# Decoder layer: the gated MLP product and the normalisation of the weighted sums on GpSimd, layer norm statistics on ScalarE, self output rows one cell later

## The chip, the cores and the metric

One core of a Trainium2 chip. Its engines are TensorE (PE in the profile, its weight loads PEld), VectorE (DVE), ScalarE (ACT), GpSimd (POOL) and SyncE (SP), which only issues DMAs here. Each has its own instruction queue and runs it in order; they meet in semaphores. The metric is the device time of one execution in microseconds, as the median of several.

## What is computed

A decoder layer in fp32 on x, 8 sequences of 512 rows by 512, with a context of the same shape. It is cut here to what matters; H = 16 heads of 32 columns, and the weights come in as they are named.

```python
x = x + self_attn(ln(x))        # q, k, v = ln(x) @ W_attn + b; q, k normed per head; causal softmax
x = x + cross_attn(ln(x), ctx)  # per row and head: the 32 largest of 512 scores, softmax over these alone
x = x + mlp(ln(x))              # below; act_quant rounds each row to 127 steps of its largest entry

def ln(x):                      # no gain, no bias
    m, v = mean(x), var(x)
    return (x - m) / sqrt(v + 1e-5)

def mlp(x):                     # w_gate, w_up: 2048 x 512, w_down: 512 x 2048, all rounded to -1, 0, 1 times a scale
    gate = silu(act_quant(x) @ w_gate.T)
    up = act_quant(x) @ w_up.T
    return act_quant(gate * up) @ w_down.T
```

## The kernel before

**Slots and cells.** One software pipeline runs over 168 slots, s = -7 to 160. Slot s works on query tile s of self attention (128 rows, one group of 4 heads: 4 tiles times 4 groups are 16 slots for each of 8 sequences) and, LAG = 20 slots later, on the same tile of cross attention. Slots repeat with a period of 16, called a batch here, and "slot 14" means s modulo 16; it begins where VectorE begins its list for s. Each slot has 8 cells, self and cross in turn, one head each. TensorE does in a cell: transposes of a head's probabilities (L595), a head's scores (L627 or L632), the weighted sum of the head before (L609), and then the shared units that `cells(s)` puts into this cell: projections for the next group (self_qkv, cross_kT, cross_v, cross_qT), the MLP's gate, up, hT and down, the output projections self_out and cross_out (L656) with the transposes ahead of them (self_oT, cross_oT), and transposes of normed rows ("feed", "x2T"). Shared units alternate between two PSUM banks, so a unit waits until the one two before it has been read. ScalarE copies each transposed block, each score block and each unit out of PSUM, cell by cell in the same order, and does the exponentials between.

**VectorE's list in a slot** is written out by hand (the loop at the end of its block). For each of the 4 cross heads it finds the 32 largest scores in 4 rounds of a maximum (L878) and a replacement (L883), in two halves of two heads, FIRST_MAX and ROUND_1 to ROUND_3, and the rest lies between: self maxima (smx), the normalisation `norms` of the finished sums (L900 reciprocal of the softmax denominators, L909 two products, so and co), `mlp` (L968 the product of silu(gate) and up into hh, L971 its row maximum), the row scale, `cross_rows` and `self_rows` (L926, L939: projection plus residual, then the statistics L929, L942 and aggregation L931, L946), `feed_stats_of` (L1000), `down` (L989). An MLP chunk is 512 of 2048 inner columns of a row tile; a tile has an early and a late chunk in each of two slots and its down projection in a third. The late chunk is worked on in the next slot, behind ROUND_1. VectorE's replacement of round 0 waits until GpSimd has done with cW of the slot before.

**GpSimd's list in a slot**: the biases cnb and snb (the negated maxima), the late chunk's silu (th, hh: L1115, L1117), the subtraction of head 2 and 3 (cS minus cW, L1170), low parts of the split operands (L1163), row quantisation, the quantisation of the inner rows (`inner_quant`, L1126, L1129, which TensorE's hT waits for), the low part of cell 3's unit, biases again, the early chunk's silu, `squares`, `head_norm` (L1146, L1149 a power, L1154; once in 4 slots, in slots 2, 6, 10 and 14), the subtraction of heads 0 and 1, and the layer norms of rows. A layer norm is four one-column instructions and a pass over 512 columns (L1049 to L1057).

**Chain around a group of heads.** In slots 2, 6, 10 and 14 TensorE forms cross_kT in cell 0 and cross_qT in cell 3; ScalarE reads each twice; GpSimd forms the low part; SyncE copies the parts into place with 8 times 4 DMAs per pair; the next slot's scores read them.

## Time and profile before

| | |
|---|---|
| time, median of 3 runs (lowest to highest) | 4032.62 us (4030.38 to 4032.80) |
| profiled execution, its time | 4034.79 us |
| its span | 4033.0 us |
| TensorE busy | 3329.4 us, 83%, 18502 matmuls |
| VectorE busy | 3343.9 us, 83% |
| ScalarE busy | 2450.5 us, 61% |
| GpSimd busy | 1796.7 us, 45% |

The span is what the trace covers; the rest of the execution's time lies around it. The first 300 us prepare weights and start the pipeline, self attention alone runs until about 425 us, six steady batches lie between 704 and 3365 us, then self attention ends, and the last 133 us hold only MLP work. A busy TensorE is not one at its peak, since its time depends on the granted clock, and a share over the whole span says little about which engine is late in a slot.

### The profile page before, as it was taken

The page shows a single profiled execution, that of the slowest core. Times are in us where ns is not written, and L with a number is a line of the kernel's source. Part 1 is how long each engine was busy: PE and PEld are TensorE (multiplying, and loading weights), DVE is VectorE, ACT ScalarE, POOL GpSimd, SP SyncE. Part 2 cuts the span into 40 slices and gives each one's busy share as a digit, 9 for nine tenths or more (in the row PEclk, how much of TensorE's full clock was granted, in tenths as well). Part 3 has the DMA queues.
Part 4 walks back from the last instruction along what each step waited for, and adds up shares of the span by engine and source line. Part 5 has one row for each costly group of instructions (what it writes and reads, how often), then busy time and mean ns, then how long its engine had stood idle before and what let it go on. Part 6 is the DMA issues. An engine that isn't in the chain of part 4 may idle for free.

```text
span 4033.0 us, 61337 instructions
## 1 busy us (share of the span) xinstructions
PE 3329.4 (83%) x18502; PEld 2434.3 (60%) x18502; DVE 3343.9 (83%) x7699; ACT 2450.5 (61%) x4921; POOL 1796.7 (45%) x2316
## 2 busy tenths in 40 slices
PE   2587898998989898998899888997899888877775
PEld 2365576666666666666666666666666666555542
DVE  4312299999999899899989999999989999999962
ACT  3344476666766567666766676666766676455533
POOL 0123244445654555444544555445544554344433
PEclk7768888888988899888988898898988898877767
DMA  7122322322222212222223222222232221211100
GB/s 271 52 54 64 99 64 76 84 77 60 77 77 72 70 49 79 79 73 69 74 77 84 63 71 67 74 65 62 77 89 79 58 66 43 61 45 35 32 21 19
DMA packets 167443, 283.04 MB, mean 70 GB/s; under 512 B 40639, under 2 KB 52939, under 8 KB 166606
## 3 DMA queue, kind: packets, MB, share of 16 engines
q1 hardware_dynamic: 160782, 275.98, 25.1%
q10 hardware_dynamic: 6336, 3.15, 0.3%
q8 instruction: 153, 2.51, 0.3%
q14 instruction: 172, 1.41, 0.1%
HBM read 113.27 MB, written 31.46 MB: 36 GB/s over the span
## 4 chain that ended last, share of the span: by engine, by line
DVE 40%; PE 25%; POOL 13%; issue 11%; ACT 4%; SPq 3%; DMA 1%; DVEq 0%; POOLq 0%; ACTq 0%
DVE cW L883 17%; DVE top L878 13%; PE bank L684 5%; PE bank L656 4%; PE bank L609 4%; POOL srs L1149 4%; SPq L513 3%; PE bank L672 2%; DVE smx L1019 2%; PE bank L637 2%; POOL cS L1170 2%; PE bank L595 2%; DVE hh L968 2%; POOL hh L1117 1%; DVE hmx L971 1%
## 5 line engine op out<-in xcount | busy, mean ns | idle before, releaser
L883 DVE MATCH_REPLACE8 cW<-top,cW 128x512 f32<-128x512 f32 x1536 | 1026.8, 676 | 0.0
L878 DVE MAX8 top<-cW 128x8 f32<-128x512 f32 x1536 | 981.4, 681 | 0.0
L799 ACT ACTIVATE PT<-bank 128x512 f32<-128x512 f32 (+3 forms) x1024 | 537.9, 525 | 356.5 <-PE bank L595 353.1
L1170 POOL TENSOR_TENSOR cS<-cS,cW 128x512 f32<-128x512 f32 x512 | 667.7, 1325 | 185.4 <-ACT cW L827 185.3
L609 PE MATMUL bank<-cv,PT 128*128 128x33 f32 x4096 | 585.0, 290 | 138.7 <-ACT PT L799 138.1
L609 PEld LDWEIGHTS bank<-cv,PT 128*128 128x128 f32 x4096 | 552.8, 209 | 176.5 <-ACT PT L799 170.2
L1177 POOL TENSOR_SCALAR cnb<-top 128x2 f32<-128x2 f32 x256 | 49.0, 191 | 938.1 <-DVE top L878 924.3
L609 PEld LDWEIGHTS bank<-sv,PT 128*128 128x128 f32 x2560 | 397.4, 211 | 82.2 <-ACT PT L799 59.6
L827 ACT ACTIVATE cW<-cW,cnb 128x512 f32<-128x512 f32 x512 | 348.7, 737 | 110.5 <-DVE cW L883 110.3
L684 PE MATMUL bank<-w_group,xT 128*128 128x384 f32 x1024 | 411.6, 550 | 0.0
L609 PE MATMUL bank<-sv,PT 128*128 128x33 f32 x2560 | 373.3, 280 | 36.7 <-ACT PT L799 35.6
L595 PE MATMUL bank<-ident,cS 128*128 128x128 f32 x2048 | 350.1, 298 | 63.2 <-POOL cS L1170 63.2
L821 ACT ACTIVATE cS<-cS,cnb 128x512 f32<-128x512 f32 x512 | 379.6, 741 | 16.1 <-DVE cW L883 16.1
L1019 DVE TENSOR_REDUCE smx<-sP 128x2 f32<-128x256 f32 (+3 forms) x256 | 205.9, 804 | 212.7 <-ACT sP L808 212.7
L1163 POOL TENSOR_TENSOR part<-part 128x512 fp32r<-128x512 f32 x128 | 168.3, 1315 | 451.1 <-ACT part L742 450.9
L595 PEld LDWEIGHTS bank<-ident,cS 128*128 128x128 f32 x2048 | 279.9, 162 | 116.7 <-POOL cS L1170 67.3
L883 DVE MATCH_REPLACE8 cW<-top,cS 128x512 f32<-128x512 f32 x512 | 342.5, 677 | 0.0
L878 DVE MAX8 top<-cS 128x8 f32<-128x512 f32 x512 | 327.2, 681 | 5.7 <-ACT cS L808 5.7
L814 ACT ACTIVATE sP<-sP,snb 128x384 f32<-128x384 f32 (+3 forms) x512 | 294.9, 578 | 35.5 <-POOL snb L1184 34.8
L808 ACT ACTIVATE cS<-bank 128x512 f32<-128x512 f32 x512 | 311.8, 609 | 1.6 <-PE bank L632 1.6
L684 PEld LDWEIGHTS bank<-w_group,xT 128*128 128x128 f32 x1024 | 205.2, 211 | 137.2 <-issue 40.3
L632 PE MATMUL bank<-ck_stack,cq_stack 128*128 128x512 f32 x512 | 269.1, 526 | 5.8 <-ACT cS L808 4.4
(151 smaller groups left out, 6092.4 us busy)
## 6 DMA issues: line engine op xcount, KB each, us to landing
sk_stack<-part SPq DMA_DIRECT2D x512, 64.0 KB, 2.0
sq_stack<-part SPq DMA_DIRECT2D x512, 64.0 KB, 2.0
ck_stack<-part SPq DMA_DIRECT2D x512, 64.0 KB, 2.0
cq_stack<-part SPq DMA_DIRECT2D x512, 64.0 KB, 2.0
w_group<-wa_by_group SPq DMA_DIRECT2D x32, 768.0 KB, 4.5
w_group<-wc_by_group SPq DMA_DIRECT2D x32, 768.0 KB, 4.3
feed<-in_x SPq DMA_DIRECT2D x32, 256.0 KB, 2.9
feed<-in_ctx SPq DMA_DIRECT2D x32, 256.0 KB, 3.0
```

Of the source, the lines that this page charges most:

```text
L595: mm = pe.transpose(turned_ps[C.parity("turned_full", label)][:, k * P:(k + 1) * P], p[:, k * P:(k + 1) * P], ident[:])
L609: mm = pe.matmul(o[:, j * (HD + 1):(j + 1) * (HD + 1)], pt[:, k * P:(k + 1) * P], v[m // NT % len(v)][:, k, j, :], start=k == 0, stop=k == ...
L684: mm = pe.matmul(ps[:, 0:3 * P], xT[:, c, t * P:(t + 1) * P], w_group[:, c, :], start=False, stop=c == NC - 1, skip_group_check=True)
L799: act.activation(PT[k][:, 0:n], turned_ps[k][:, 0:n], ACT.Copy).then_inc(turned_read, step("turned_read", label))
L808: act.activation(dst, score_ps[k][:, 0:n], ACT.Copy).then_inc(score_read, step("score_read", label))
L814: act.activation(p, p, ACT.Exp, bias=snb[:, j:j + 1], scale=SCALE).then_inc(sexp, step("sexp", (m, j)))
L821: act.activation(cS[c % 2][j][:], cS[c % 2][j][:], ACT.Exp, bias=cnb[c % 2][:, j:j + 1], scale=SCALE).then_inc(cexp, step("cexp", (c, j)))
L827: act.activation(cW[j][:], cW[j][:], ACT.Exp, bias=cnb[c % 2][:, j:j + 1], scale=SCALE).then_inc(crest, step("crest", (c, j)))
L878: dve.max(top8[:, j, r, :], src[:]).then_inc(topk, step("topk", (c, r, "max", j)))
L883: dve.match_replace(cW[j][:], top8[:, j, r, :], src[:], REPLACED).then_inc(topk, step("topk", (c, r, "replace", j)))
L1019: dve.reduce_max(smx[:, 2 * half:2 * half + 2], sP[half][:, :, 0:n], AXX).then_inc(smax, step("smax", (s, half)))
L1170: pool.tensor_tensor(cS[m % 2][j][:], cS[m % 2][j][:], cW[j][:], ALU.subtract).then_inc(cprob, step("cprob", (m, j)))
```

## The change

- GpSimd takes the product of silu(gate) and up (third instruction of `silu`), early and late chunk; VectorE keeps the row maximum. ScalarE's next read of an up bank waits for GpSimd in place of VectorE.
- ScalarE copies both finished weighted sums and denominators from PSUM to a new SBUF tile oc (`copy_out`, cell 1). VectorE takes the reciprocals from there (`inverses`), GpSimd forms so and co (`normalise`), ahead of the subtraction of heads 2 and 3. TensorE may reuse the PSUM bank after the copy.
- The row statistics of all layer norms move to ScalarE: a copy with an accumulated sum, a tiny scaling to the negative mean, and a square with an accumulated sum. They stand in cells 4 and 5 (cross rows), 4 and 6 (feeds of the next slot), 6 and 7 (self rows). GpSimd's layer norm loses two one-column instructions.
- self_oT and self_out move from cells 2 and 3 to 3 and 4, the transpose of the x1 rows from cell 1 to 2, cross_qT from cell 3 to 4. VectorE's `self_rows` stands behind ROUND_1 of the second half. GpSimd handles the low parts of cells 3 and 4 together.
- SyncE stores a slot's rows and loads those of the next at the end of the slot, behind the copies of the parts, with the xres load last; feeds are loaded behind these. x1res is the same buffer as xres.

```diff
-        for at, cell, unit in ((1, 5, ("cross_v", g)), (2, 0, ("cross_kT", g)), (2, 3, ("cross_qT", g))):
+        for at, cell, unit in ((1, 5, ("cross_v", g)), (2, 0, ("cross_kT", g)), (2, 4, ("cross_qT", g))):
...
-        u[1].append(("feed", "x1", x1_tile(s)))
+        u[2].append(("feed", "x1", x1_tile(s)))
-        u[2].append(("self_oT", self_tile(s)))
-        u[3].append(("self_out", self_tile(s)))
+        u[3].append(("self_oT", self_tile(s)))
+        u[4].append(("self_out", self_tile(s)))
...
+            def row_stats_of(s, k):
+                out = []
+                if k in (4, 5) and cross_tile(s) is not None:
+                    out.append((("x2", cross_tile(s)), x2t, x2sum, (0, 1) if k == 4 else (2,)))
+                if k in (4, 6):
+                    for f in feeds(s + 1):
+                        if f[0] == "x":
+                            out.append((f, feed[ring[f] % RING], fsum[normed.index(f) % RING], (0, 1) if k == 4 else (2,)))
+                if k in (6, 7) and self_tile(s) is not None:
+                    out.append((("x1", self_tile(s)), xres, x1sum, (0, 1) if k == 6 else (2,)))
+                return out
...
+                        if on(s - 3) or on(s - LAG - 3):
+                            pe.wait_ge(out_copied, upto("out_copied", s - 1))
...
-                                act.wait_ge(h_dve, upto("h_dve", ("h", *prev)))
+                                act.wait_ge(h_pool, upto("h_pool", ("h", *prev)))
...
+                    def copy_out(s):
+                        m, c = s - 2, s - LAG - 2
+                        if not on(m) and not on(c):
+                            return
...
+                        o = out_ps[s % 2][:].rearrange("p (k n) -> p k n", k=2)
+                        act.activation(oc[:, first:last, :], o[:, first:last, 0:HG * (HD + 1)], ACT.Copy).then_inc(
+                            out_copied, step("out_copied", s))
+                    def statistics(s, k):
+                        for label, x_, sums_, steps in row_stats_of(s, k):
+                            if 0 in steps:
+                                if label[0] == "x2":
+                                    act.wait_ge(dve_rows, upto("dve_rows", label))
+                                elif label[0] == "x1":
+                                    act.wait_ge(x1_added, upto("x1_added", label[1]))
+                                    act.wait_ge(x1_norm, upto("x1_norm", (label[1] - 1, 2)))
+                                else:
+                                    act.wait_ge(feed_in[ring[label] % RING], upto(f"feed_in{ring[label] % RING}", label, 16))
+                                    p = normed.index(label)
+                                    if p >= RING:
+                                        act.wait_ge(feed_pool, upto("feed_pool", (normed[p - RING], 2)))
+                                if label[0] == "x2":
+                                    act.wait_ge(pool_rows, upto("pool_rows", ("ln", label[1] - 1, 3)))
+                                act.wait_ge(row_stats, upto("row_stats", (label, 0)) - 1)
+                                act.activation(junk[:], x_[:], ACT.Copy, accum_out=sums_[:, 0:1]).then_inc(
+                                    row_stats, step("row_stats", (label, 0)))
+                                act.wait_ge(row_stats, upto("row_stats", (label, 0)))
+                                act.activation(sums_[:, 1:2], sums_[:, 0:1], ACT.Copy, scale=-1.0 / D).then_inc(
+                                    row_stats, step("row_stats", (label, 1)))
+                            else:
+                                act.wait_ge(row_stats, upto("row_stats", (label, 2)) - 1)
+                                act.activation(junk[:], x_[:], ACT.Square, bias=sums_[:, 1:2], accum_out=sums_[:, 2:3]).then_inc(
+                                    row_stats, step("row_stats", (label, 2)))
...
-                        if on(m):
-                            dve.wait_ge(so_full, upto("so_full", m))
-                        if on(c):
-                            dve.wait_ge(co_full, upto("co_full", c))
+                        o = oc[:].rearrange("p k (h d) -> p k h d", h=HG)
+                        dve.wait_ge(out_copied, upto("out_copied", s))
                         dve.wait_ge(so_norm, upto("so_norm", m - 1))
                         dve.wait_ge(co_norm, upto("co_norm", c - 1))
                         dve.reciprocal(rr[:, first:last, :], o[:, first:last, :, HD]).then_inc(recip, step("recip", s))
-                        dve.wait_ge(recip, upto("recip", s))
-                        for k, n, o_t, unit in ((0, m, so, "self_oT"), (1, c, co, "cross_oT")):
-                            if not on(n):
-                                continue
...
-                            mult = dve.tensor_tensor(o_t[:, qt, g * P:(g + 1) * P].rearrange("p (h d) -> p h d", h=HG),
-                                                     o[:, k, :, 0:HD], rr[:, k, :].unsqueeze(2).to_broadcast([P, HG, HD]),
-                                                     ALU.mult)
...
...
-                        dve.wait_ge(dve_rows, upto("dve_rows", ("x2", t)))
-                        dve.bn_stats(mstat[:], x2t[:]).then_inc(dve_rows, step("dve_rows", ("stats", t)))
-                        dve.wait_ge(dve_rows, upto("dve_rows", ("stats", t)))
-                        dve.bn_aggr(mv[:], mstat[:]).then_inc(dve_rows, step("dve_rows", ("aggr", t)))
...
-                            dve.wait_ge(h_pool, upto("h_pool", ("r", t, n)))
-                            dve.wait_ge(shared_read, upto("shared_read", (("up", t, n), 0)))
-                            dve.tensor_tensor(hh[:, n, :], hh[:, n, :], uc[:], ALU.mult).then_inc(
-                                h_dve, step("h_dve", ("h", t, n)))
-                            dve.wait_ge(h_dve, upto("h_dve", ("h", t, n)))
+                            dve.wait_ge(h_pool, upto("h_pool", ("h", t, n)))
...
+                        top(c, 1, ROUND_1)
                         self_rows(s)
-                        top(c, 1, ROUND_1)
-                        feed_stats_of(s + 1)
...
-                    def layer_norm(dst, src, mvt, col, name, sem_, label, ready):
+                    def layer_norm(dst, src, sums_, col, name, sem_, label, ready):
 
                         ready()
-                        pool.tensor_scalar(col[:, 0:1], mvt[:, 1:2], 1.0, EPS, ALU.mult, ALU.add).then_inc(sem_, step(name, label(0)))
+                        pool.tensor_scalar(col[:, 0:1], sums_[:, 2:3], 1.0 / D, EPS, ALU.mult, ALU.add).then_inc(sem_, step(name, label(0)))
                         pool.wait_ge(sem_, upto(name, label(0)))
                         pool.tensor_tensor(col[:, 1:2], col[:, 0:1], minus_half[:, 0:1], ALU.pow).then_inc(sem_, step(name, label(1)))
                         pool.wait_ge(sem_, upto(name, label(1)))
-                        pool.tensor_tensor(col[:, 2:3], mvt[:, 0:1], col[:, 1:2], ALU.mult).then_inc(sem_, step(name, label(2)))
-                        pool.wait_ge(sem_, upto(name, label(2)))
-                        pool.tensor_scalar(col[:, 3:4], col[:, 2:3], -1.0, 0.0, ALU.mult, ALU.add).then_inc(sem_, step(name, label(3)))
-                        pool.wait_ge(sem_, upto(name, label(3)))
-                        return pool.tensor_scalar(dst, src, col[:, 1:2], col[:, 3:4], ALU.mult, ALU.add)
+                        return pool.tensor_scalar(dst, src, sums_[:, 1:2], col[:, 1:2], ALU.add, ALU.mult)
...
+                    def normalise(s):
+                        m, c = s - 2, s - LAG - 2
+                        o = oc[:].rearrange("p k (h d) -> p k h d", h=HG)
+                        for k, n, o_t, name in ((0, m, so, "self_oT"), (1, c, co, "cross_oT")):
+                            if not on(n):
+                                continue
+                            b, qt, g = n // SLOTS, n % NT, n // NT % NG
+                            pool.wait_ge(recip, upto("recip", s))
+                            if b and g == 0:
+                                pool.wait_ge(shared_full, upto("shared_full", (name, NT * (b - 1) + qt)))
+                            mult = pool.tensor_tensor(o_t[:, qt, g * P:(g + 1) * P].rearrange("p (h d) -> p h d", h=HG),
+                                                      o[:, k, :, 0:HD], rr[:, k, :].unsqueeze(2).to_broadcast([P, HG, HD]),
+                                                      ALU.mult)
+                            if k == 0:
+                                mult.then_inc(so_norm, step("so_norm", n))
+                            else:
+                                mult.then_inc(co_norm, step("co_norm", n))
...
+                            pool.wait_ge(h_pool, upto("h_pool", ("r", t, n)))
+                            pool.wait_ge(shared_read, upto("shared_read", (("up", t, n), 0)))
+                            pool.tensor_tensor(hh[:, n, :], hh[:, n, :], uc[:], ALU.mult).then_inc(
+                                h_pool, step("h_pool", ("h", t, n)))
...
+                        normalise(s)
                         for j in (2, 3):
                             probability(c - 1, j)
                         low_parts(now[0] + now[1] + now[2])
                         rows_quant(s)
                         inner_quant(s - 1)
-                        low_parts(now[3])
+                        low_parts(now[3] + now[4])
```

On VectorE, the second half of slot 14, from the end of the first half on. Before:

```order
L878 MAX top<-cW 128x8 x2
L883 MATCH_REPLACE cW<-top,cW 128x512 x2
L878 MAX top<-cS_2 128x8
L878 MAX top<-cS_3 128x8
L1019 TENSOR_REDUCE smx<-sP 128x2
L939 TENSOR_TENSOR xres<-bank,xres 128x512
L942 BN_STATS x1stat<-xres 128x6
L946 BN_AGGR x1mv<-x1stat 128x2
L883 MATCH_REPLACE cW<-top,cS_2 128x512
L883 MATCH_REPLACE cW<-top,cS_3 128x512
L878 MAX top<-cW 128x8 x2
L883 MATCH_REPLACE cW<-top,cW 128x512 x2
```

After:

```order
L943 MATCH_REPLACE cW<-top,cW 128x512 x2
L938 MAX top<-cS_2 128x8
L938 MAX top<-cS_3 128x8
L1032 TENSOR_REDUCE smx<-sP 128x2
L943 MATCH_REPLACE cW<-top,cS_2 128x512
L943 MATCH_REPLACE cW<-top,cS_3 128x512
L938 MAX top<-cW 128x8 x2
L976 TENSOR_TENSOR xres<-bank,xres 128x512
L943 MATCH_REPLACE cW<-top,cW 128x512 x2
L938 MAX top<-cW 128x8 x2
L998 TENSOR_REDUCE hmx<-hh 128x1
L943 MATCH_REPLACE cW<-top,cW 128x512 x2
```

The add of the self output moves behind the first replacement and maximum of this half, and the two statistics instructions behind it are gone.

On GpSimd, the start of slot 13 up to the quantisation of the inner rows (hcol, hh). Before:

```order
L1177 TENSOR_SCALAR cnb<-top 128x2
L1184 TENSOR_SCALAR snb<-smx 128x2
L1115 TENSOR_SCALAR th<-th 128x512
L1117 TENSOR_TENSOR hh<-th,hh 128x512
L1170 TENSOR_TENSOR cS_2<-cS_2,cW 128x512
L1170 TENSOR_TENSOR cS_3<-cS_3,cW 128x512
L1126 TENSOR_TENSOR hcol<-hcol,wscale 128x1
L1129 TENSOR_SCALAR hh<-hh,hcol 128x512 x4
```

After:

```order
L1208 TENSOR_SCALAR cnb<-top 128x2
L1215 TENSOR_SCALAR snb<-smx 128x2
L1142 TENSOR_SCALAR th<-th 128x512
L1144 TENSOR_TENSOR hh<-th,hh 128x512
L1148 TENSOR_TENSOR hh<-hh,uc 128x512
L1099 TENSOR_TENSOR so<-oc,rr 128x128
L1099 TENSOR_TENSOR co<-oc,rr 128x128
L1201 TENSOR_TENSOR cS_2<-cS_2,cW 128x512
L1201 TENSOR_TENSOR cS_3<-cS_3,cW 128x512
L1157 TENSOR_TENSOR hcol<-hcol,wscale 128x1
L1160 TENSOR_SCALAR hh<-hh,hcol 128x512 x4
```

Three instructions stand between the silu's second step and the subtraction of head 2 that weren't there.

On TensorE, slot 14, cells 2 to 4, from the transposes of probabilities of cell 2 on; cross_qT is the line with x1T, self_out those with ones and wproj. Before:

```order
L595 MATMUL bank<-ident,sP 128x128 x2
L627 MATMUL bank<-sk_stack,sq_stack 128x384
L629 MATMUL bank<-mask,ident 128x128
L609 MATMUL bank<-cv,PT 128x33 x4
L637 MATMUL bank<-ident,so 128x128 x4
L595 MATMUL bank<-ident,cS_1 128x128 x4
L632 MATMUL bank<-ck_stack,cq_stack 128x512
L609 MATMUL bank<-sv,PT 128x33 x2
L703 MATMUL bank<-x1T,w_group 128x512 x4
L653 MATMUL bank<-bias,ones 128x512
L656 MATMUL bank<-wproj,oT 128x512 x4
L595 MATMUL bank<-ident,sP 128x128 x2
```

After:

```order
L610 MATMUL bank<-ident,cS_1 128x128 x4
L647 MATMUL bank<-ck_stack,cq_stack 128x512
L624 MATMUL bank<-sv,PT 128x33 x2
L652 MATMUL bank<-ident,so 128x128 x4
L610 MATMUL bank<-ident,sP 128x128 x2
L642 MATMUL bank<-sk_stack,sq_stack 128x384
L644 MATMUL bank<-mask,ident 128x128
L624 MATMUL bank<-cv,PT 128x33 x4
L718 MATMUL bank<-x1T,w_group 128x512 x4
L668 MATMUL bank<-bias,ones 128x512
L671 MATMUL bank<-wproj,oT 128x512 x4
```

The transpose of so follows cell 3's own work in place of cell 2's, and cross_qT and self_out follow cell 4's.

## Rows read from the trace of the kernel before

**Rows 1.** Stretches: us; busy PE, PEld, DVE, ACT, POOL; clock; DMA.

```profile
2478.00:2922.00 444.00, 392.51 (x2285) 289.66 (x2284) 409.13 (x946) 296.68 (x606) 225.54 (x289) 0.90 0.27 72
...
3700.00:3900.00 200.00, 141.26 (x637) 102.61 (x638) 189.17 (x448) 97.14 (x166) 73.14 (x86) 0.68 0.08 22
```

**Rows 2.** Timeline of DVE, slot 14 of two batches: start, duration, [idle before].

```profile
2490.11 0.69 DVE L939 TENSOR_TENSOR xres<-bank,xres 128x512 f32<-128x512 f32 x1 [4.95 <-PE bank L656]
...
2933.85 0.69 DVE L939 TENSOR_TENSOR xres<-bank,xres 128x512 f32<-128x512 f32 x1 [4.95 <-PE bank L656]
```

**Rows 3.** Waits of DVE, 2478 to 2922: us in total, times, longest.

```profile
DVE xres L939 <- PE bank L656: 13.9, 4, 5.6
DVE x2res L989 <- PE bank L672: 5.8, 4, 2.2
...
DVE cW L883 <- POOL cS L1170: 3.3, 3, 2.3
```

**Rows 4.** Waits of PE, the same stretch.

```profile
PE bank L637 <- POOL hh L1129: 19.6, 4, 8.7
PE bank L595 <- POOL cS L1170: 8.3, 3, 5.1
```

**Rows 5.** The chain of waits by line, the same stretch.

```profile
by line: DVE cW L883 15.9%; DVE top L878 12.4%; issue 11.3%; PE bank L684 5.6%; PE bank L609 5.5%; POOL srs L1149 4.9%; PE bank L656 4.5%; PE bank L595 3.1%; POOL cS L1170 3.1%; DVE smx L1019 2.6%; DVE hh L968 2.4%; PE bank L672 2.4%; PE ba
```

**Rows 6.** Groups of DVE instructions, the same stretch: busy us, mean ns, idle before.

```profile
L968 DVE TENSOR_TENSOR hh<-hh,uc 128x512 f32<-128x512 f32 x16 | 16.1, 1008 | 3.0 <-POOL hh L1117 3.0
...
L909 DVE TENSOR_TENSOR so<-bank,rr 128x128 f32<-128x128 f32 x16 | 4.7, 292 | 0.5
...
L942 DVE BATCH_NORM_STATS2 x1stat<-xres 128x6 f32<-128x512 f32 x4 | 2.8, 695 | 0.1
...
L946 DVE BATCH_NORM_AGGREGATE x1mv<-x1stat 128x2 f32<-128x6 f32 x4 | 0.7, 182 | 0.1
```

**Rows 7.** Timeline of POOL, start of a slot 13 to the quantisation.

```profile
2447.25 0.19 POOL L1184 TENSOR_SCALAR snb<-smx 128x2 f32<-128x2 f32 x1
2447.52 0.62 POOL L1115 TENSOR_SCALAR th<-th 128x512 f32<-128x512 f32 x1
2448.22 1.27 POOL L1117 TENSOR_TENSOR hh<-th,hh 128x512 f32<-128x512 f32 x1
2449.45 2.94 POOL L1170 TENSOR_TENSOR cS<-cS,cW 128x512 f32<-128x512 f32 x2
2452.64 0.19 POOL L1126 TENSOR_TENSOR hcol<-hcol,wscale 128x1 f32<-128x1 f32 x1 [0.26 <-DVE hcol L982]
```

**Rows 8.** Groups, whole span: a broadcast product, an ACT copy, the accumulator read.

```profile
L1154 POOL TENSOR_TENSOR sx<-sx,srs 128x1024 f32<-128x1024 f32 x32 | 62.0, 1937 | 2.5
...
L742 ACT ACTIVATE sx<-bank 128x256 f32<-128x256 f32 x128 | 48.9, 382 | 269.3 <-PE bank L684 268.9
...
L1398 ACT ACTIVATION_READ_ACCUMULATOR scratch<-wnat 128x1 f32 x12 | 2.3, 192 | 0.0
```

**Rows 9.** Timeline of POOL, slot 14: low part, power, subtraction.

```profile
2487.50 1.27 POOL L1163 TENSOR_TENSOR part<-part 128x512 fp32r<-128x512 f32 x1 [9.19 <-ACT part L742]
...
2491.52 5.45 POOL L1149 TENSOR_TENSOR srs<-srs,minus_half 128x32 f32<-128x32 f32 x1
...
2499.08 2.50 POOL L1170 TENSOR_TENSOR cS<-cS,cW 128x512 f32<-128x512 f32 x2
```

**Rows 10.** Timeline of DVE near the end: the product beside GpSimd, and alone.

```profile
3564.49 1.28 DVE L968 TENSOR_TENSOR hh<-hh,uc 128x512 f32<-128x512 f32 x1
...
4016.85 0.69 DVE L968 TENSOR_TENSOR hh<-hh,uc 128x512 f32<-128x512 f32 x1 [1.99 <-POOL hh L1117]
```

**Rows 11.** Timeline of PE, slots 13 to 15.

```profile
2453.65 1.09 PE L637 MATMUL bank<-ident,hh 128*128 128x128 f32 x4 [5.13 <-POOL hh L1129]
...
2489.91 0.38 PE L595 MATMUL bank<-ident,sP 128*128 128x128 f32 x2
...
2491.24 0.63 PE L595 MATMUL bank<-ident,cS 128*128 128x128 f32 x4
...
2500.40 0.66 PE L595 MATMUL bank<-ident,cS 128*128 128x128 f32 x4 [0.74 <-POOL cS L1170]
```

184 lines of the change are left out of this document (81 added, 103 removed).

## The prediction

> **What bounds the kernel now.** I read the table of stretches first. In a steady batch of 16 slots VectorE is busy 409 of 444 us, TensorE 393 at a mean granted clock of 0.90, ScalarE 297 and GpSimd 226 [rows 1]. So two engines are nearly full, and two have room. The period is 2933.85 - 2490.11 = 443.74 us, the distance of the same instruction in two batches [rows 2]. The engine waits come next: VectorE's largest is 13.9 us for the self output rows, then 5.8 us for the down projection and 3.3 us for GpSimd's subtraction [rows 3]; TensorE's are 19.6 us for the quantised MLP rows and 8.3 us for the same subtraction [rows 4]. Last the chain of waits: in this batch it is on VectorE's top-32 lines for 28% only, the rest is spread over TensorE lines and over GpSimd's power, 4.9% [rows 5]. The chain hops from engine to engine, so work taken from VectorE pays only in the stretches where VectorE is the one that is late. That is how I cost the change: engine by engine, along the chain.
>
> **What leaves VectorE.** Per batch: 16 multiplications by the up rows at 1.01 us (16.1 us), 32 normalising multiplications at 0.29 but 0.21 apart in the queue (6.6 us), 12 times statistics and aggregation, 0.70 + 0.18 less their overlap, 0.83 (10 us) [rows 6]. Sum 32.7 us per batch. That would be the gain if nothing else bound anything.
>
> **What the other engines get.** GpSimd's product of 512 columns is 1.27 us, with the gap to the next 1.35 [rows 7]; that is the price of each moved multiplication. The normalising product (128 columns, a broadcast operand) is not in the trace. Its nearest rows are the broadcast product of 1024 columns at 1.94 us and a two-column GpSimd instruction at 0.19 us [rows 7, 8]; on the line between them 128 columns cost 0.41. I take 0.41, with 0.19 and 0.62 (the one-input pass over 512 columns [rows 7]) as ends. Two of them and their gaps: 1.0 us per slot. Each layer norm loses two tiny GpSimd instructions, 0.55 us with gaps. ScalarE gets a copy of 264 columns from PSUM per slot, 0.38 as its copy of 256 [rows 8], and per tile two passes over 512 columns with an accumulator read of 0.19 each [rows 8] and one tiny one: about 0.6 + 0.19 twice, plus 0.25, 1.85 us, 12 times a batch. That is 28 us on an engine that has 147 us idle per batch, so by itself I cost it at nothing; what covers it is that ScalarE mostly waits for TensorE. If that cover is gone (the three feed tiles in one cell, 3 us at once) it costs a TensorE wait of 1 to 2 us.
>
> **A rule against the trace.** When a subtraction of two tiles on GpSimd overlaps VectorE's multiplication, the pair of them takes 2.94 us; alone it takes 2.50 [rows 7, 9]. VectorE's multiplication is 0.69 alone and 1.28 beside GpSimd [rows 10]. The top-32 instructions never show it. So I credit 0.45 us per late chunk to GpSimd once VectorE's two-input product is gone. The Trainium skill, page "SBUF — State Buffer", section "Who interferes with whom", says that a VectorE instruction with two SBUF inputs contends with a GpSimd instruction that reads SBUF and one with a single input does not; by it the relief is the one that I take from the rows. The page "Perfetto Trace Analysis", section "Optimizing Scalar/DVE Operations", warns that moving work between these two engines might not help; the rival that it stands for is priced below as B from rows.
>
> **The chain leg by leg, one batch.** Numbers are change against before; minus is gained.
>
> Slots 8 and 9, VectorE never waits. Two early multiplications (1.4 beside GpSimd, 0.7 alone), the norms of slot 8 (0.4), three feed statistics (2.8 with their gaps) and one late chunk. The late chunk pays little: VectorE (replacement, maximum, reciprocal) would be ready 2.7 us after its self maxima, GpSimd (bias, two silu steps, the new product) 3.6 us after them, by the steps of [rows 7]; so 0.9 us of the 1.4 for norms and product turns into a wait, and 0.5 is left. Sum -5.8.
>
> Slot 10 takes that back. Its quantisation hangs on GpSimd: from the bias at 2447.25 to the scale at 2452.64 that queue has 0.26 us of idle time in it, in slot 13's example [rows 7]. The new product (1.35) and the two norms (1.0), less 0.45 and less the wait, put the first quantised rows 1.7 us later; TensorE waits for them in every such slot, 5.13 us in this one [rows 11]. Then cross_qT comes a cell later. A cell's own work is 1.33 us at the full clock (2489.91 to 2491.24) [rows 11], and twice that at the lower of the two clock levels, 1.2 instead of 2.4 GHz, to which the granted clock has fallen after such a wait (four transposes take 1.09 there and 0.63 at the full level). Behind cross_qT hang ScalarE's read, GpSimd's low part, the head norm with its 5.45 us power and 1.95 us product, and the subtraction for head 0, which the next slot's VectorE and TensorE both need: GpSimd runs this without idle time from 2487.50 to 2501.6 [rows 9], and TensorE waits 0.74 for it [rows 11]. At the start of slot 11 I expect about +0.5: leg +6.3.
>
> Slots 11 and 12, VectorE again: two early (1.4), one late (0.5), norms (0.4), one feed (0.8): -3.1.
>
> Slot 13: quantisation, +1.7. Slot 14: cross_qT a cell later, +1.35, and the early product ahead of the head norm, +1.35; with the pair 2.8 to 2.9, I take +2.85 with its larger gap.
>
> Slot 15: the layer norm is shorter (-0.55), the early product is off VectorE (-0.7), the self output comes a cell later (+1.5 with its unit), but VectorE now does its replacement and maximum (2.5 us) before it waits and has no statistics after it (0.83): -3.35. Sum -3.1. In slot 14 the same gain is void, since GpSimd is late there.
>
> Slot 0: quantisation, +1.7. Slots 1 and 2: self output and norms, +1.5 - 3.35 - 0.4 = -2.25. Slots 3 and 4 are TensorE and the SyncE copies: 0.
>
> Slots 5 to 7: VectorE gains 3.9 up to the cross rows of slot 6 (norms 0.4, statistics 0.9, early product 1.0, and the late chunk of slot 6 in full, 1.6, since the sum of squares gives GpSimd time), but TensorE was waiting only 2.3 us for them, so -2.3; then cross_qT +1.5, the early product +1.35, layer norm -0.55, late product -0.5. Sum -0.5.
>
> Total: -5.8 + 6.3 - 3.1 + 1.7 + 2.85 - 3.1 + 1.7 - 2.25 - 0.5 = -2.2 us per batch. Six batches lie between 704 and 3365 us: -13. Ahead of them there is no MLP and SyncE's copies and TensorE lead; I put 0, within 5.
>
> **The end.** From 3426 to 3900 us only the cross attention and MLP run; VectorE is busy 189 of 200 us, TensorE 141 [rows 1], and there is no head norm. Here the saving comes through: 8 early multiplications at 0.9, 8 late ones at 0.5 (the 1.28 beside GpSimd [rows 10] becomes a wait for it), four row statistics 3.5, norms 2.4; less 1 for the down slots: -16. In the last 133 us nothing covers a hop. Per tile the last chunk's product is 1.35 on GpSimd for 0.70 on VectorE [rows 10]: +2.6 in four tiles; three layer norms whose sums come through ScalarE, about +1 each: +5.6 in all. Net -10.4.
>
> SyncE's list is the same in its order around the copies but that feeds are issued behind the row loads and that x1res shares the buffer of xres; the tiles of the two are slots apart, and I cost it at 0.
>
> **Sum.** -13 - 10.4 = -23.4 us, against the profiled execution's 4034.8 (its span is 4033.0 and 1.8 lie around it) that is 4011; against the median of 4032.6 it is 4009. I say 4010.
>
> **Rivals.** *A, the legs have slack.* If engines upstream of the q leg run so much earlier that its later cell doesn't show, the four q legs (6 us) and the quantisation (5 us) go: -13 per batch, -78 and the end's -10: about 3945. For it: only 8.3 us of waits per batch are put to the subtraction [rows 4]. Against: GpSimd has no idle time in that leg [rows 9]. The full 32.7 us cannot come: TensorE's 393 us and even half of its 51 us of idle time are more than the 411 that would be left.
>
> *B, GpSimd becomes the bound (slower).* If each q leg starts in the low clock (+2.7, not +1.35), and if the layer norm of the x1 rows, which must now wait for ScalarE's last cell and stands ahead of the next slot's biases, pushes silu and quantisation by 2 to 3 us in slots 15 and 0, a batch costs 4 x 1.35 + 3 - 2.2 = +6.2, six of them +37, the end -10: about 4060. It decides from +1.7 per batch on, where it eats the end's gain. For it: GpSimd's unbroken run [rows 9] and the 19.6 us that TensorE waits for quantised rows [rows 4]. Against: GpSimd is busy only 226 of 444 us [rows 1].
>
> *C, it only trades places.* Late chunks: VectorE waits where it worked, which I priced; if the early ones do the same, and legs and gains cancel, the time is 4033 within 8.
>
> **How the numbers follow.** Forecast (4010, own range 3985 to 4024) 0.40; A 0.12; C 0.19; B 0.29. The unknown product moves a quantisation leg by 0.4 either way, 1.2 per batch, 7 in all. The range holds A at its low end and B at its high end: 3945 to 4060. A measurement of this kernel can tell about 0.2% from no change. Faster by more: 0.40 + 0.12, rounded to 0.51; within: 0.20; slower: 0.29.
>
> **What would show it.** Right: a period near 441.5 in the middle; VectorE busy 377 of it with its waits up from 32 to about 60; TensorE's wait for the quantised rows up by 1.5 us a slot; the subtraction for heads 2 and 3 at 2.50 a pair; GpSimd's normalising product near 0.4 us; the power's start in slot 14 later against cross_kT by 2.8. A is right if the waits for the subtraction don't grow, B if they double and the clock's mean falls below 0.88. Wrong altogether: ScalarE copies of the transposed weights delayed by the statistics so that TensorE waits for them by more than 10 us a batch, or a GpSimd product beside the top-32 work that takes much more than 1.3 us.

## The result: slower by 2.6%

The changed kernel takes 4137.30 us in the median (4131.15 to 4139.49), the kernel before 4031.50 beside it: a ratio of 1.0261, interval 1.0243 to 1.0278. I had said 4010, with 4060 as the end of the range. The profiled executions have spans of 4133.7 and 4033.0 us. One execution of the kernel before and one of undo_cells took 5954 and 5998 us and stand apart from all others; without its own, the median of undo_cells is 4123.2 in place of the 4125.5 below.

A batch, 16 slots from one slot 4 to the next, in the table of stretches of the changed kernel (the columns of [rows 1]):

```profile
2255.70:2713.10 457.40, 403.12 (x2285) 298.81 (x2285) 376.10 (x874) 317.61 (x681) 245.90 (x312) 0.89 0.26 70
```

VectorE is busy 376 us where it was 409 [rows 1], as foretold (377). But the batch has become 13.5 us longer. VectorE's and TensorE's waits in it, against [rows 3] and [rows 4]:

```profile
DVE rr L956 <- ACT oc L858: 28.8, 12, 5.2
DVE x2res L1016 <- PE bank L687: 13.8, 4, 4.3
DVE hmx L998 <- POOL hh L1148: 13.1, 7, 3.8
DVE xres L976 <- PE bank L671: 11.6, 3, 8.7
DVE cW L943 <- POOL cS L1201: 7.8, 8, 2.5
...
PE bank L652 <- POOL hh L1160: 20.2, 4, 7.7
...
PE bank L610 <- POOL cS L1201: 12.2, 4, 5.0
```

VectorE now waits 81 us a batch where it waited 32. The largest wait is new: 28.8 us in 12 slots for ScalarE's copy of the weighted sums, ahead of the reciprocals. The second new one is 13.1 us for GpSimd's product. The chain of waits of the same stretch has moved off VectorE's top-32 lines, from 28% [rows 5] to 13%:

```profile
by line: issue 8.7%; PE bank L624 7.4%; DVE cW L943 7.3%; PE bank L699 6.9%; DVE top L938 5.8%; PE bank L671 5.3%; POOL cS L1201 4.1%; PE bank L610 4.1%; POOL srs L1180 3.6%; PE bank L687 3.1%; PE bank L718 3.1%; PE bank L652 3.0%; PE bank 
```

Where in the batch the time is: below are slot lengths, each the distance between VectorE's first maxima (top<-cS) of two slots, the median over five batches; for the other kernels the difference to before. They are worked out from the timelines of VectorE; the kernels after the second column are those of the experiments. Some slots jump between two lengths from batch to batch, so medians of slots do not add up to a batch: as the mean of the same five batches the bottom line would be +13.7, +2.0, +6.2, +2.7, -2.9, -5.2, -3.7 and -10.0.

```
slot   before   changed   undo_norm  copy_early    early_x1      q_back    no_cells    hh_stats hh_stats_x1
0        34.6      +6.8        +6.0        +6.9        +0.3        +1.4        -1.5        +4.8        -2.2
1        23.6      +0.8        -0.9        -0.2        -1.0        -1.0        -0.6        +0.2        -0.6
2        23.3      +1.8        +0.0        -0.1        -0.1        -0.1        -0.6        +0.0        +0.0
3        26.0      +1.3        +4.6        +4.1        +5.8        +4.6        +2.4        +1.3        +2.1
4-7     119.1      +0.4        +0.2        +0.5        -0.8        -1.1        -1.6        -1.4        -1.4
8-9      51.7      -4.0        -5.5        -5.3        -5.3        -5.3        -5.3        -5.5        -5.5
10       27.6      +6.5        +1.7        +4.0        +5.5        +3.1        +3.1        +2.7        +2.7
11-12    50.8      -0.2        -1.7        -2.3        -2.3        -2.5        -2.5        -2.8        -2.8
13       25.1      +2.6        -1.0        +0.9        +3.8        -0.5        -0.5        -1.0        -0.9
14       31.2      -3.2        -3.8        -3.5        -3.5        -3.6        -1.7        -1.9        -1.9
15       30.5      +0.8        +0.3        +1.0        +1.0        -1.0        +0.4        +0.4        +0.4
sum     443.4     +13.7         0.0        +6.0        +3.3        -6.0        -8.3        -3.2       -10.3
```

Of the 100.7 us between the two spans, 0.9 lie ahead of the first slot with cross attention, 14.2 in the first batch after it (slots that have no MLP work), 82.2 in the six full batches, 0.1 in the next 15 slots and 3.3 behind them.

**Slot 10** shows the new wait at work. ScalarE, VectorE, GpSimd and TensorE in the timeline of the changed kernel (start, duration, instruction, [idle before <- what ended it]); the slot begins at 2423.23:

```profile
2423.54 1.92 PE L624 MATMUL bank<-cv,PT 128*128 128x33 f32 x8 [2.55 <-ACT PT L814]
2425.27 6.04 PE L718 MATMUL bank<-ctxT,w_group 128*128 128x512 f32 x8
...
2425.51 1.34 ACT L842 ACTIVATE cW<-cW,cnb 128x512 f32<-128x512 f32 x2
2431.34 1.27 ACT L757 ACTIVATE part<-bank,ccol 128x512 fp32r<-128x512 f32 x2 [4.49 <-PE bank L718]
...
2433.45 0.41 ACT L858 ACTIVATE oc<-bank 128x264 f32<-128x264 f32 x1
...
2433.89 0.20 DVE L956 RECIPROCAL rr<-oc 128x8 f32<-128x8 f32 x1 [5.17 <-ACT oc L858]
...
2434.18 0.40 POOL L1099 TENSOR_TENSOR so<-oc,rr 128x128 f32<-128x128 f32 x1 [3.17 <-DVE rr L956]
2434.53 0.40 POOL L1099 TENSOR_TENSOR co<-oc,rr 128x128 f32<-128x128 f32 x1
2434.89 2.50 POOL L1201 TENSOR_TENSOR cS<-cS,cW 128x512 f32<-128x512 f32 x2
...
2438.75 2.70 POOL L1160 TENSOR_SCALAR hh<-hh,hcol 128x512 f32<-128x512 f32 x4
```

The last product of the weighted sums (bank<-cv,PT, cell 0) starts at 2423.54 and is over before 2425.5. ScalarE is free at 2426.9. But the copy is in its cell 1, behind the reads of cross_kT, for which ScalarE stands still 4.49 us. VectorE stands 5.17 us for the copy, GpSimd 3.17 us for VectorE's reciprocal, and the subtraction and the quantised rows (2438.75, 15.5 us into the slot; before 8.8) are queued behind that. One late copy holds three queues.

Part of these 5.17 us is VectorE's own lead. Counted from the start of slot 8, ScalarE reads cross_kT after 54.8 us in the kernel before and after 55.9 in the changed one, but VectorE is ready for its reciprocal after 57.2 and 53.3: what it saved in slots 8 and 9 it stands for in slot 10. In the kernel before there would have been next to no wait here, since the score read ahead of the place of the copy ends at 2372.37, just before the reciprocal starts:

```profile
2371.76 0.61 ACT L808 ACTIVATE cS<-bank 128x512 f32<-128x512 f32 x1
...
2372.45 0.20 DVE L900 RECIPROCAL rr<-bank 128x8 f32<-128x8 f32 x1
```

**Slot 0** shows another. The timeline of GpSimd at the end of slot 15 and the start of slot 0 (2594.93):

```profile
2589.61 2.51 POOL L1201 TENSOR_TENSOR cS<-cS,cW 128x512 f32<-128x512 f32 x2 [1.31 <-ACT cW L842]
2599.03 0.19 POOL L1061 TENSOR_SCALAR x1col<-x1sum 128x1 f32<-128x1 f32 x1 [6.92 <-ACT junk L885]
...
2600.81 0.19 POOL L1208 TENSOR_SCALAR cnb<-top 128x2 f32<-128x2 f32 x1
...
2607.84 2.69 POOL L1160 TENSOR_SCALAR hh<-hh,hcol 128x512 f32<-128x512 f32 x4
```

The layer norm of the x1 rows waits 6.92 us for the sums that ScalarE forms in its cells 6 and 7, and slot 0's biases, silu, product and quantisation stand behind it. The quantised rows come 12.9 us into slot 0; in the kernel before it is 8.1.

**The granted clock** is in these lengths too. Here are two slots 13 of one kernel, early_x1 of the experiments below, in the table of stretches (the columns of [rows 1]), and TensorE's wait in each:

```profile
2005.32:2029.85 24.53, 22.86 (x166) 18.63 (x164) 23.09 (x57) 16.43 (x39) 14.30 (x19) 1.00 0.11 33
2448.47:2477.30 28.83, 25.22 (x148) 20.86 (x148) 22.99 (x57) 14.82 (x35) 14.31 (x19) 0.82 0.09 28
...
2014.75 0.63 PE L652 MATMUL bank<-ident,hh 128*128 128x128 f32 x4 [1.67 <-POOL hh L1160]
...
2457.87 1.09 PE L652 MATMUL bank<-ident,hh 128*128 128x128 f32 x4 [3.61 <-POOL hh L1160]
```

VectorE and GpSimd do the same work in both. Where TensorE waited 1.67 us for the quantised rows its clock stayed at the upper level of 2.4 GHz; where it waited 3.61 us the clock fell, to a mean of 0.82 of it, and the slot is 4.3 us longer for 1.9 us more of waiting. The wait isn't all that decides: in a slot 13 of q_back (from 2429.21) it is 1.7 us, and the clock has a mean of 0.88 and the slot 27.7 us. What tips the clock is not shown. Weighted by slot lengths, the mean granted clock of the five batches is 0.893 before, 0.880 in the changed kernel and 0.906 in hh_stats_x1, the fastest below. If all of the shortfall is time at the lower level of 1.2 GHz, that is an estimate of 94, 109 and 81 us of a batch. How much of the 13.7 us is the clock's no run separates.

### The profile page after: what moved, and what is told of

It reads as the page before. It is cut to its first block, busy times and chain, and to the rows that moved or that the text cites. A ratio compares the mean times of both kernels' runs of the same rounds, so it can differ in the third digit from the quotient of the medians.

```text
span 4133.7 us, 61724 instructions
## 1 busy us (share of the span) xinstructions
PE 3405.0 (82%) x18502; PEld 2499.2 (60%) x18502; DVE 3081.9 (75%) x7123; ACT 2623.7 (63%) x5549; POOL 1970.0 (48%) x2508
## 4 chain that ended last, share of the span: by engine, by line
PE 36%; DVE 20%; POOL 16%; ACT 12%; issue 9%; SPq 2%; DMA 1%; DVEq 0%; ACTq 0%; POOLq 0%
DVE cW L943 9%; DVE top L938 8%; PE bank L699 7%; PE bank L624 6%; PE bank L671 5%; PE bank L610 3%; POOL srs L1180 3%; POOL cS L1201 3%; PE bank L652 3%; PE bank L687 3%; PE bank L718 3%; PE bank L711 2%; POOL hh L1144 2%; SPq L528 2%; ACT PT L814 2%
## 5 line engine op out<-in xcount | busy, mean ns | idle before, releaser
L624 PE MATMUL bank<-cv,PT 128*128 128x33 f32 x4096 | 603.9, 295 | 171.3 <-ACT PT L814 170.2
L1201 POOL TENSOR_TENSOR cS<-cS,cW 128x512 f32<-128x512 f32 x512 | 641.2, 1274 | 172.1 <-ACT cW L842 172.0
L624 PEld LDWEIGHTS bank<-cv,PT 128*128 128x128 f32 x4096 | 567.6, 214 | 215.5 <-ACT PT L814 211.1
L624 PEld LDWEIGHTS bank<-sv,PT 128*128 128x128 f32 x2560 | 413.4, 218 | 88.1 <-ACT PT L814 62.5
L699 PE MATMUL bank<-w_group,xT 128*128 128x384 f32 x1024 | 426.3, 567 | 0.0
L624 PE MATMUL bank<-sv,PT 128*128 128x33 f32 x2560 | 384.1, 286 | 42.6 <-ACT PT L814 41.8
```

Of the source, the lines that this page charges most:

```text
L624: mm = pe.matmul(o[:, j * (HD + 1):(j + 1) * (HD + 1)], pt[:, k * P:(k + 1) * P], v[m // NT % len(v)][:, k, j, :], start=k == 0, stop=k == ...
L699: mm = pe.matmul(ps[:, 0:3 * P], xT[:, c, t * P:(t + 1) * P], w_group[:, c, :], start=False, stop=c == NC - 1, skip_group_check=True)
L1201: pool.tensor_tensor(cS[m % 2][j][:], cS[m % 2][j][:], cW[j][:], ALU.subtract).then_inc(cprob, step("cprob", (m, j)))
```

## Experiments

All times are medians, ratios are to the kernel before on the same chip; the kernel before had 4035 to 4039 there, so a difference in us between kernels of different groups holds to some 5 us. Single runs of one kernel lie up to 14 us off its median, so differences of 10 us or less between two kernels are not read.

### One part of the change alone, on the kernel before

**add_hh**: the product.

```diff
+                            pool.tensor_tensor(hh[:, n, :], hh[:, n, :], uc[:], ALU.mult).then_inc(
...
-                            dve.tensor_tensor(hh[:, n, :], hh[:, n, :], uc[:], ALU.mult).then_inc(
```

> The kernel before, with only the product of silu(gate) and up moved to GpSimd. Theory 1 (the 105 us come from queues in order: each part makes one engine wait inside its list, and what stands behind pays): GpSimd's quantised rows come about 1 us later in each of the four late chunks that are quantised, the four power legs 1.3 us later, against 8 early multiplications of VectorE that pay in full; 4025 to 4045. Theory 2 (only the parts together are slow, since GpSimd's list overflows): within 0.2% of the kernel before. Theory 3 (GpSimd's products themselves are what costs): at least half of the 105 us, over 4080.

Measured 4019.9, ratio 0.9955 (0.994 to 0.9969). **add_norm**: copy, reciprocals, products.

```diff
-                        norms(s)
+                        inverses(s)
...
                         elif k == 1:
+                            copy_out(s)
...
+                        normalise(s)
```

> The kernel before, with only ScalarE's copy of the weighted sums, VectorE's reciprocal from it and GpSimd's normalising products. In the changed kernel VectorE waits 28.8 us per batch for that copy, a wait that was not there before. Theory 1: the copy stands in ScalarE's cell 1 behind work for which VectorE never waited; VectorE's reciprocal waits 1 to 2 us in most slots and what GpSimd has behind it (subtraction, quantisation) moves with it: 20 to 50 us slower, 4050 to 4080. Theory 2: within 0.2% of the kernel before, since the waits of VectorE are only a symptom of being late elsewhere. Theory 3: 10 us slower at most.

Measured 4064.3, ratio 1.0065 (1.0048 to 1.0081). **add_stats**: the row statistics.

```diff
-                        dve.bn_stats(mstat[:], x2t[:]).then_inc(dve_rows, step("dve_rows", ("stats", t)))
...
+                            statistics(s, k)
```

> The kernel before, with only the row statistics on ScalarE, in the cells where the changed kernel has them. Theory 1: GpSimd's layer norm of the x1 rows waits for ScalarE's cell 7 in slots 15, 0, 1 and 2 (6.9 us of idle time in one such slot of the changed kernel) and stands ahead of the next slot's biases and silu: 3 to 4 us per such slot with an MLP chunk behind it, 10 us a batch less the 10 us that VectorE saves in part: 4040 to 4080. Theory 2: VectorE's 10 us a batch come through in part: 4000 to 4030. Theory 3: same as theory 2.

Measured 4026.5, ratio 0.9969 (0.9956 to 0.9982). **add_cells**: the units and rows that are moved.

```diff
-        for at, cell, unit in ((1, 5, ("cross_v", g)), (2, 0, ("cross_kT", g)), (2, 3, ("cross_qT", g))):
+        for at, cell, unit in ((1, 5, ("cross_v", g)), (2, 0, ("cross_kT", g)), (2, 4, ("cross_qT", g))):
-        u[1].append(("feed", "x1", x1_tile(s)))
+        u[2].append(("feed", "x1", x1_tile(s)))
-        u[2].append(("self_oT", self_tile(s)))
-        u[3].append(("self_out", self_tile(s)))
+        u[3].append(("self_oT", self_tile(s)))
+        u[4].append(("self_out", self_tile(s)))
...
+                        top(c, 1, ROUND_1)
                         self_rows(s)
-                        top(c, 1, ROUND_1)
...
-                        low_parts(now[3])
+                        low_parts(now[3] + now[4])
```

> The kernel before, with only the units moved a cell later (self_oT, self_out, the transpose of the x1 rows, cross_qT) and VectorE's self output rows behind the second half's first round. Theory 1: four power legs a cell later cost 1.35 to 2.7 us each, and four waits of VectorE for the self output (13.9 us a batch before) get 1 us shorter each: 4030 to 4065. Theory 2: within 0.2%. Theory 3: within 0.2%. Over 4080 would say that the moves of the cells alone make most of the loss.

Measured 4064.3, ratio 1.0071 (1.0054 to 1.0087). So two parts gain (-19 and -13 us) and two lose (+25 each, against the 4039 beside them). Together that is +18; the whole change gave +106. For add_stats theory 1 was wrong, and for add_hh it was 5 us too high at its lower end; the rest had to be sought in how parts meet.

### One part of the change undone

The edits are those above, turned round.

> The changed kernel with the shared units back in the cells of the kernel before (self_oT, self_out, the x1 transpose, cross_qT) and VectorE's self output rows back ahead of the second half's first round. The four parts alone gave -19, +25, -13 and +25 us, a sum of +18 where the whole change gave +106, so some 88 us lie in how parts meet. Theory 1 (self output rows a cell later and ScalarE's statistics meet: the rows come later and the statistics in cells 6 and 7 with the layer norm behind them then delay the next slot's silu): most of the 88 us go with this part, 4020 to 4060. Theory 2 (the copy of the weighted sums meets the rest): only its own 25 us go, 4100 to 4120.

> The changed kernel with the normalisation back on VectorE, from PSUM. Theory 1: its own 25 us go and a little more, 4085 to 4115. Theory 2: the copy in ScalarE's cell 1 is what turns every lateness of GpSimd (late biases, late exponentials) into a wait of VectorE and back into GpSimd's list; without it the loop is open and 60 us or more go: 4030 to 4075.

> The changed kernel with the row statistics back on VectorE. Theory 1: GpSimd's layer norm of the x1 rows no longer waits 6.9 us for ScalarE; VectorE gets 10 us of work a batch back; 40 to 80 us faster than the changed kernel, 4060 to 4095. Theory 2: the statistics alone gained 13 us, so they cost that to undo: 4135 to 4155.

Measured: without the cell moves 4125.5 (ratio 1.022, 1.0203 to 1.0237), without the normalisation 4050.9 (1.0036, 1.0022 to 1.005), without the statistics 4091.4 (1.0146, 1.0129 to 1.0163). Both theories on the cells missed: dear alone, they give 12 us when undone (17 by the ratios). Undoing the normalisation gives 86 us. The table says where: slot 10 falls from +6.5 to +1.7, slot 13 from +2.6 to -1.0. These are slots in which inner rows are quantised.

Undoing the statistics gives 46 us, though alone they had gained 13. With them VectorE's wait for the copy goes as well, from 28.8 to 14.8 us a batch (alone, in add_norm, it is 10.6), while undoing the cells leaves it at 28.8:

```profile
DVE rr L915 <- ACT oc L845: 14.8, 10, 3.1
```

So the copy and the statistics meet: about half of the wait for the copy is there only beside the statistics. Whether ScalarE's longer list does it, or the lead that VectorE gets by them, no run separates.

**x1ln_late** was meant to take the wait of slot 0 out of the way of the next slot's silu.

```diff
                         inner_quant(s - 1)
+                        x1_ln(s - 1)
...
-                        x1_ln(s)
```

> The changed kernel with one call moved in GpSimd's list: the layer norm of the x1 rows stands behind the next slot's quantisation of the inner rows and no longer at the end of its own slot, so biases and silu don't wait behind ScalarE's statistics. Theory 1: slots 0 to 2 and 15 lose 3 to 5 us where a late chunk follows, 5 to 10 us a batch: 4070 to 4110. Theory 2: the wait only moves to TensorE's transpose of the same rows in cell 2, within 10 us of the changed kernel, 4127 to 4147.

Measured 4294.8, ratio 1.0639 (1.0623 to 1.0655): both theories wrong. TensorE's list has the transpose of these rows in cell 2, and it now waits for them, a wait that the changed kernel doesn't have (waits of TensorE, 2200 to 2675 us):

```profile
PE bank L652 <- POOL rown L1065: 20.2, 4, 7.2
PE bank L652 <- POOL hh L1160: 15.7, 3, 7.7
```

### The place of the copy, and of the statistics

**copy_early** is the changed kernel with the copy in ScalarE's cell 0.

```diff
                             rest_exp(c - 1, 3)
+                            copy_out(s)
                         elif k == 1:
-                            copy_out(s)
```

> The changed kernel with ScalarE's copy of the weighted sums at the end of its cell 0, ahead of its reads of that cell's units, and not in cell 1. The last matrix product of these sums is in TensorE's cell 0, ahead of cross_kT; in slot 10 of the changed kernel it ends at 2425.5 us, but the copy comes at 2433.5, behind the reads of cross_kT, and VectorE stands 5.2 us. Theory 1 (the place of the copy in ScalarE's list is what makes the normalisation dear): VectorE's 28.8 us of waits for the copy per batch all but go, slots 10 and 13 lose 3 to 5 and 2 us, 8 to 13 us a batch: 4050 to 4085. Theory 2 (what is dear are the products that GpSimd has ahead of its subtraction, the copy only shows it): within 20 us of the changed kernel, 4115 to 4137.

Measured 4087.2, ratio 1.0122 (1.0102 to 1.0142): 50 us faster than the changed kernel by a line moved. VectorE's wait for the copy falls from 28.8 to 7.2 us a batch:

```profile
DVE rr L956 <- ACT oc L858: 7.2, 5, 2.0
```

and in slot 10 (from 2389.4) the copy comes before ScalarE's idle time, not behind it (ScalarE, then VectorE):

```profile
2394.23 0.39 ACT L858 ACTIVATE oc<-bank 128x264 f32<-128x264 f32 x1
2398.75 1.26 ACT L757 ACTIVATE part<-bank,ccol 128x512 fp32r<-128x512 f32 x2 [4.12 <-PE bank L718]
...
2394.84 0.20 DVE L956 RECIPROCAL rr<-oc 128x8 f32<-128x8 f32 x1
```

The first batch, which has no MLP work, shrinks from 404.6 to 387.4 us (before: 390.4), so its 14 us were the copy's too. **norm_early**: the same line moved in add_norm.

> The kernel before with the normalisation moved alone, and the copy in ScalarE's cell 0. With the copy in cell 1 it was 25 us slower than the kernel before, with 10.6 us of waits for the copy per batch. Theory 1: 4025 to 4045. Theory 2: 4055 to 4070, as with the copy in cell 1.

Measured 4022.2, ratio 0.9956 (0.9941 to 0.9971), where add_norm had 1.0065. In this kernel the same part, with its copy a cell earlier, gains 15 us where it lost 25. Theory 1 holds twice in its mechanism; both times lie 2 to 3 us outside its range.

**early_x1**: copy_early with the x1 statistics a cell earlier.

```diff
-                if k in (6, 7) and self_tile(s) is not None:
-                    out.append((("x1", self_tile(s)), xres, x1sum, (0, 1) if k == 6 else (2,)))
+                if k in (5, 6) and self_tile(s) is not None:
+                    out.append((("x1", self_tile(s)), xres, x1sum, (0, 1) if k == 5 else (2,)))
```

> The kernel of the run before it with the statistics of the x1 rows in ScalarE's cells 5 and 6, one cell earlier. In slot 15 the rows are added at 2588.1 us, ScalarE's cell 5 ends at about 2590.5 and its cell 7 at 2599: GpSimd's layer norm waited 6.9 us for it. Theory 1: GpSimd's biases and silu of slot 0 come 3 to 5 us earlier, slot 0 loses most of its 6.8 us: 15 to 40 us faster than the run before it. Theory 2 (slot 0 is late by something else, such as the self output rows a cell later): within 5 us of it.

Measured 4070.9, ratio 1.0084 (1.0068 to 1.0101). Slot 0 falls from +6.9 to +0.3; slots 3, 10 and 13 take 6 of these 6.6 us a batch back, though slots 10 and 13 jump between two lengths; the whole is 16 us faster. **hh_stats** has only the product and the statistics, **hh_stats_x1** also the x1 statistics a cell earlier.

> The kernel before with the product of silu(gate) and up on GpSimd and the row statistics on ScalarE, the two parts that were faster alone (-19 and -13 us). If parts add: 4003 to 4012 where the kernel before has 4036 to 4039. If the two meet (GpSimd's layer norm of the x1 rows waits for ScalarE while the products make its list longer): 4015 to 4035.

> The kernel hh_stats (product on GpSimd and statistics on ScalarE, 4021) with the statistics of the x1 rows in ScalarE's cells 5 and 6. In hh_stats slot 0 is 4.8 us longer than before, and GpSimd waits 23.7 us a batch for these statistics. Theory 1: slot 0 loses 4 us, 24 us in six batches: 3990 to 4003. Theory 2 (the moved statistics delay ScalarE's copies for TensorE in cells 5 and 6 as much): 4012 to 4025.

Measured 4020.8 (0.9957, 0.994 to 0.9973) and 3986.7 (0.9876, 0.9861 to 0.9892): the two parts didn't add (4007 expected), and one cell for the x1 statistics gave 34 us. GpSimd at the end of slot 15, first in hh_stats (slot 0 at 2519.6), then in hh_stats_x1 (slot 0 at 2503.2):

```profile
2522.74 0.19 POOL L1061 TENSOR_SCALAR x1col<-x1sum 128x1 f32<-128x1 f32 x1 [6.91 <-ACT junk L867]
...
2524.51 0.19 POOL L1188 TENSOR_SCALAR cnb<-top 128x2 f32<-128x2 f32 x1
```

```profile
2504.15 0.19 POOL L1061 TENSOR_SCALAR x1col<-x1sum 128x1 f32<-128x1 f32 x1 [4.72 <-ACT junk L867]
...
2505.92 0.19 POOL L1188 TENSOR_SCALAR cnb<-top 128x2 f32<-128x2 f32 x1
...
2512.27 2.69 POOL L1140 TENSOR_SCALAR hh<-hh,hcol 128x512 f32<-128x512 f32 x4
```

The bias comes 4.9 us into slot 0 in the one and 2.7 us in the other. GpSimd still waits 4.72 us there, but of that only 1.3 us reach slot 0: in the kernel before this bias comes 1.4 us into it.

### What was left: the cells, SyncE's order, the rest

> The kernel early_x1 (copy in ScalarE's cell 0, statistics of the x1 rows in cells 5 and 6) with the shared units and VectorE's self output rows back where the kernel before has them; early_x1 took 4071. Theory 1 (with the copy and the statistics mended, what is left over the kernel before is the price of the moved cells, 25 us alone, and the three moves of work gain again as they did alone): 3985 to 4015, below both kernels. Theory 2 (what is left lies in SyncE's new order or in GpSimd's longer list): 4040 to 4065.

> The kernel early_x1 with cross_qT alone back in cell 3 (and GpSimd's low part with it); self_oT, self_out, the x1 transpose and the self output rows stay a cell later. The prediction charged the cell of cross_qT 1.35 to 2.7 us per power leg, four a batch, and credited the later self output. If the q legs carry the cost: 4035 to 4055, most of the way to no_cells. If the self output carries it (slot 3 is 5.8 us longer in early_x1 than before, and cross_qT isn't near it): within 10 us of early_x1, 4060 to 4080.

> The kernel before with only SyncE's list in the new order and x1res in the buffer of xres. The prediction put it at 0. Theory 1: within 10 us of the kernel before, 4027 to 4047. Theory 2 (stores and loads behind the copies of the parts come late, feeds too): over 4050.

Measured: **no_cells** (early_x1 with all units in their old cells) 4008.7 (0.9932, 0.9917 to 0.9947); **q_back** (early_x1 with cross_qT alone in cell 3 again) 4027.9 (0.9973, 0.9959 to 0.9987); **add_sync** (the kernel before with SyncE's new order and the shared buffer) 4030.7 (0.999, 0.998 to 0.9999). So SyncE's order costs nothing. The cells cost 62 us here, 43 of them cross_qT (q_back is 7 us under the range expected for it). There are 32 units cross_qT, 4 for each of 8 sequences, which makes 1.3 us for each in the mean. The other 19 us, from q_back to no_cells, are the self output and the transposes: a cell later they make slots 14 and 15 shorter, by 1.9 and 1.4 us, but slots 0 and 3 longer, by 2.9 and 2.2. In slot 14 of early_x1 the power begins 22.9 us into the slot and the subtraction 30.3, in q_back 21.0 and 28.4:

```profile
2500.18 5.44 POOL L1180 TENSOR_TENSOR srs<-srs,minus_half 128x32 f32<-128x32 f32 x1
...
2507.57 2.50 POOL L1201 TENSOR_TENSOR cS<-cS,cW 128x512 f32<-128x512 f32 x2
```

```profile
2477.92 5.44 POOL L1180 TENSOR_TENSOR srs<-srs,minus_half 128x32 f32<-128x32 f32 x1
...
2485.31 2.50 POOL L1201 TENSOR_TENSOR cS<-cS,cW 128x512 f32<-128x512 f32 x2
```

(The first from early_x1, the second from q_back; their slots 14 begin at 2477.3 and 2456.9.) The slot itself takes 27.6 us in both; the time is in slots 15, 10 and 3 (2.0, 2.4 and 1.2 us by the table) and in slot 13, which jumps with the clock as shown above. In the changed kernel itself undoing all the cells gave 12 us only. My reading is that the copy and the x1 statistics were later than they were, and hid them; no run undoes the cells with only one of the two mended.

Two last runs started from the best kernels. **norm_behind** is no_cells with the two products behind the subtraction; **late_max** is hh_stats_x1 with VectorE's row maximum of chunk 1 behind its round 2.

```diff
-                        normalise(s)
                         for j in (2, 3):
                             probability(c - 1, j)
+                        normalise(s)
```

> The kernel no_cells (4009) with GpSimd's two normalising products behind its subtractions of heads 2 and 3 and no longer ahead of them. no_cells differs from hh_stats_x1 (3987) by the normalisation on GpSimd, ScalarE's copy of the sums and SyncE's order; alone, with the copy in cell 0, the normalisation gained 15 us. Theory 1 (in GpSimd's list the products, and the wait for VectorE's reciprocal of 17 us a batch, keep the subtraction back, which VectorE and TensorE wait for): 3990 to 4003. Theory 2 (what the two kernels differ in is ScalarE's longer list, or chance in how the stretches fall): within 6 us of no_cells, 4003 to 4015.

```diff
-                        mlp(s - 1, False)
+                        if (NF - 1) in [n for _, n in mlp_chunk(s - 1, False)]:
+                            mlp(s - 1, False)
                         top(c, 0, ROUND_2)
+                        if (NF - 1) not in [n for _, n in mlp_chunk(s - 1, False)]:
+                            mlp(s - 1, False)
```

> The kernel hh_stats_x1 (3987) with VectorE's row maximum of a late chunk behind its round 2 and not ahead of it, in the slots where no quantisation follows (chunk 1 of 0 to 3). VectorE waits 14.1 us a batch for GpSimd's product in 8 slots, four of them such slots. Theory 1: VectorE is what is late in slots 8, 9, 11 and 12, so the wait of some 1.8 us goes into the time there: 5 to 7 us a batch less, 3950 to 3970. Theory 2: in half of these slots another engine is as late: 3970 to 3982. Theory 3: no change, within 5 us.

Measured 3999.9 (0.9909, 0.9891 to 0.9928) and 3997.7 (0.9902, 0.9885 to 0.9919). The first is 9 us better than no_cells, in the range of its theory 1 but inside what I don't read: why the kernel with the normalisation is 22 us slower than hh_stats_x1 isn't settled. The second missed all three theories: it is 11 us slower. VectorE's wait for the product did fall, from 14.1 to 11.1 us a batch, but its waits for TensorE's self output rose from 11.9 to 18.1 and for the row loads from 5.5 to 10.7, and slot 0 is 3.7 us longer (waits of VectorE in late_max, 2200 to 2640 us):

```profile
DVE xres L976 <- PE bank L669: 18.1, 4, 6.8
DVE hmx L998 <- POOL hh L1131: 11.1, 6, 3.4
DVE x2t L967 <- DMA x1res<-x_rows: 10.7, 2, 5.5
```

hh_stats_x1, at 3986.7, beats the kernel before by 1.2% and the changed one by 3.6%. Its batch, from one slot 4 to the next:

```profile
2176.50:2610.00 433.50, 390.38 (x2287) 288.20 (x2288) 383.04 (x906) 312.72 (x665) 234.56 (x280) 0.92 0.27 74
```

TensorE's clock of 0.92, up from 0.90 [rows 1], goes with the shorter waits for quantised rows (11.5 us a batch, before 19.6 [rows 4]).

## Why the prediction was wrong

Right, by its own steps:

- **The unit prices.** The normalising product took 0.40 (0.41 taken), GpSimd's product 1.27, the subtraction of a pair 2.50 once VectorE's two-input product was gone (2.94 before), ScalarE's statistics of a tile 0.62 + 0.19 + 0.20 + 0.72 + 0.19 = 1.9 (1.85). VectorE lost 33 us of work a batch (32.7). By the Trainium skill, page "SBUF — State Buffer", section "Who interferes with whom", the relief of the subtraction was to be expected, and the trace agrees (2.50 a pair; no single subtraction of the changed kernel takes over 1.30 us, where 59 of 512 took up to 1.74 before).
- **The quantisation and power legs, in part.** The prediction gave slot 10 +6.3, which is the -5.8 of slots 8 and 9 taken back and 0.5 more; it measured +6.5. That agreement is chance: slots 8 to 10 together were +0.5 foretold and +2.5 measured, and the wait for the copy was in it (5.17 us). The cell of cross_qT was priced at 1.35 to 2.7 us a leg; it cost 1.3 in the mean, and the power's start in slot 14 is 2.3 us later against cross_kT (2.8 foretold). But slot 14 was to be 2.85 longer and is 3.2 shorter: the gain of the later self output rows, declared void there, came through, and the leg shows in slot 15 (-3.1 foretold, +0.8 measured). Of its other signs, VectorE's waits became 81 us and not 60, and TensorE's for the quantised rows hardly grew (19.6 to 20.2).
- **SyncE's order** at 0: the run with it alone was 0.1% off the kernel before.

Wrong:

- **"On an engine that has 147 us idle per batch, so by itself I cost it at nothing."** This is the step that failed. What I added to ScalarE was short (0.4 us a slot for the copy, 1.9 a tile), and it did fit into its idle time. But ScalarE is idle inside its list, waiting for TensorE cell by cell, and what stands behind such a wait comes that much later. I asked whether the copy has room, never when its result comes and who needs it: I had written VectorE's reciprocal and GpSimd's products down at their durations, with no wait for the copy at all. That wait was 28.8 us a batch. The copy's place alone made 50 us of the 106; with the copy one cell earlier the part that had lost 25 us gained 15.
- **The x1 statistics.** Rival B named the mechanism (the layer norm waits for ScalarE's last cell and stands ahead of silu and quantisation) and priced it at 2 to 3 us in slots 15 and 0. The wait was 6.9 us, slot 0 grew by 6.8 where the forecast had +1.7. One cell earlier gave 16 us with the other faults still there, and 34 without them. I had the place but took its delay from a guess about cells, though the trace of the kernel before had the times: in slot 15 GpSimd comes to this layer norm at 2526.91 and ScalarE ends its cell 7 at 2532.12, 5.2 us later, to which the last statistics are added (GpSimd, then the last instruction of ScalarE's cell 7):

```profile
2526.91 0.19 POOL L1049 TENSOR_SCALAR x1col<-x1mv 128x1 f32<-128x1 f32 x1
...
2531.39 0.73 ACT L814 ACTIVATE sP<-sP,snb 128x512 f32<-128x512 f32 x1
```

- **The self output rows a cell later** were credited with 1.85 us net in slot 15 and again in slots 1 and 2. Moving them and the transposes back gave 19 us (q_back to no_cells): their gain is in slots 14 and 15, and slots 0 and 3 take more than that back.
- **The gain in slots 11, 12, 1 and 2**: -5.35 foretold, +2.4 measured. In slots 12, 1 and 2 VectorE waited 2.1 to 2.6 us for the copy in the batch shown, in slot 11 not at all. With the copy early and the x1 statistics early, 11 and 12 gave -2.3 of the -3.1, 1 and 2 gave -1.1 of the -2.25.
- **The end**: -10.4 foretold. The +3.4 above (0.1 and 3.3) counts from 3512 us of the kernel before; from 3355 us on, about where the forecast's end begins, it is +8.0. From 3525 to 3955 us VectorE waits 14.5 us for the copy and 12.8 for the product, which take back most of what it saved (415 us busy in the matching stretch before, 383 here). Behind that VectorE waits 2.72 to 4.87 us for the product of each of the last chunks, but it waited 1.99 to 3.61 there before, and two products of one tile are 3.41 us apart in both kernels: the +2.6 foretold for them isn't seen.

```profile
DVE rr L956 <- ACT oc L858: 14.5, 4, 4.5
DVE hmx L998 <- POOL hh L1148: 12.8, 9, 3.2
```

- **The start** was put at 0 within 5; it was +14, and the copy's.
- **The range.** B was the right side, but its upper end was worked out from two of the three late queues. A wait that doesn't exist before has no row in the trace of before, but a part of it can be worked out there, by laying the place of the copy in ScalarE's list beside VectorE's reciprocal. In slot 4 that gives 3.4 us and the copy's 0.4 (add_norm measured 3.19):

```profile
2200.92 0.19 DVE L900 RECIPROCAL rr<-bank 128x8 f32<-128x8 f32 x1
...
2203.69 0.61 ACT L808 ACTIVATE cS<-bank 128x512 f32<-128x512 f32 x1
```

Over the 16 slots it gives an estimate of 13 us a batch, where add_norm measured 10.6. The other 18 of the 28.8 us are not in the trace of before, the 5.17 of slot 10 least of all: they come with the other parts, and 14 go when the statistics are undone.

## What to carry to other kernels

An instruction that is moved to an engine with idle time costs no more than it lasts only if nobody waits for its result. Look at where in that engine's list it stands, and add every wait of the list ahead of it up to the point; then look at what stands behind the consumer. What the old trace gives for a new wait can be far too small where the change also moves the consumer earlier or the producer later (13 us a batch against 28.8). The cheapest place found here is right behind the event that makes the input ready, ahead of the next wait: that was one line, worth 50 us. And a part that seems cheap in a slow kernel (the cells, 12 us) can be dear (62 us) in a mended one: undo parts in the order of what is latest, and measure again.

## What the runs showed that I had not expected

Costs of parts were far from adding: alone -19, +25, -13 and +25, together +106; undoing the normalisation gave 86 us, over three times what adding it had cost. The same moved line was worth 42 us on the kernel before and 50 on the changed one. Moving one layer norm half a list later in GpSimd's queue cost 157 us, some 17 us of it in each steady batch, where TensorE's new wait is 20.2 us and its wait for the quantised rows 4.5 us shorter: hardly anything of the new wait was hidden by others.
